# Two-layer transformer: a sequence's value sums are turned and divided in two steps instead of one

## What is computed

```python
# layer 0: 16 heads of 16, every head with its own keys and values
attn = jax.nn.softmax(jnp.einsum('gqd,gkd->gqk', q, k) * norm, axis=-1)
ctx = jnp.einsum('gqk,gkd->gqd', attn, v)
out = ctx @ Wproj.T + bproj
# layer 1: 16 heads, 4 groups of keys and values, causal
scores = jnp.where(causal[None, None, :, :], -jnp.inf, scores)
attn = jax.nn.softmax(scores, axis=-1)
out = jnp.einsum('bhqk,bhkd->bhqd', attn, v)
```

## Time and profile before

| | us |
|---|---|
| median of 3 runs | 715.38 |
| lowest and highest run | 715.2, 718.11 |
| the profiled execution (its span) | 734.3 |
| PE busy in it | 556.6 (76%) |
| DVE busy | 478.0 (65%) |
| ACT busy | 340.3 (46%) |
| POOL busy | 262.3 (36%) |

### The profile page before, as it was taken

One profiled execution on the slowest core, in us unless ns is written; L12 is line 12 of the kernel. 1 busy time (PEld: TensorE's weight loads), 2 busy tenths in 40 slices (PEclk: granted clock), 3 DMA queues, 4 the chain that ended last, 5 costly groups with the idle time before them and its releaser, 6 DMA issues.

```text
span 734.3 us, 14600 instructions
## 1 busy us (share of the span) xinstructions
PE 556.6 (76%) x4098; PEld 390.8 (53%) x4099; DVE 478.0 (65%) x1351; ACT 340.3 (46%) x870; POOL 262.3 (36%) x398
## 2 busy tenths in 40 slices
PE   4996669899796789788787877765589999899100
PEld 2653435565486555556565654543277777677100
DVE  4558548686158883757674852665757777677488
ACT  2541437577655546145653554530055555555100
POOL 1431001001411134245345243455436666566400
PEclk9997789999998899889989797866799999999655
DMA  7779967400000019693033051162434444444392
GB/s 222 197 245 243 215 135 211 141 2 4 1 1 1 1 55 246 162 241 139 3 112 137 16 203 53 37 244 88 130 96 138 143 145 143 136 140 134 130 409 84
DMA packets 50397, 95.19 MB, mean 130 GB/s; under 512 B 8676, under 2 KB 40620, under 8 KB 48556
## 3 DMA queue, kind: packets, MB, share of 16 engines
q1 hardware_dynamic: 41516, 71.14, 34.2%
q0 software_dynamic: 7680, 19.21, 7.1%
q10 hardware_dynamic: 1152, 4.19, 1.4%
HBM read 58.54 MB, written 35.59 MB: 128 GB/s over the span
## 4 chain that ended last, share of the span: by engine, by line
PE 47%; DVE 24%; DMA 7%; issue 7%; ACT 6%; another core or an unknown queue 4%; POOL 2%; SPq 1%; ACTq 0%; DVEq 0%; POOLq 0%
PE banks L1462 9%; PE banks L1252 5%; PE banks L1477 5%; DMA arena<-negT 4%; DVE arena L2029 4%; PE banks L1085 4%; PE banks L1208 4%; PE banks L1273 3%; DVE mx L1757 3%; DVE mx L1760 2%; PE banks L1449 2%; PE banks L1091 2%; PE banks L1153 2%; PE banks L1367 1%
## 5 line engine op out<-in xcount | busy, mean ns | idle before, releaser
L958 ACT ACTIVATE arena<-banks 128x512 f32<-128x512 f32 (+1 forms) x256 | 130.8, 547 | 118.7 <-PE banks L1252 75.7
L1252 PE MATMUL banks<-arena 98*128 98x256 bf16 (+1 forms) x512 | 93.5, 279 | 44.4 <-DMA arena<-negT 18.2
L1757 DVE TENSOR_REDUCE mx<-banks 128x4 f32<-128x1024 f32 x64 | 76.1, 1221 | 32.9 <-PE banks L1208 32.9
L1208 PE MATMUL banks<-arena 96*128 96x256 bf16 (+1 forms) x512 | 91.5, 285 | 6.0 <-DVE mx L1757 3.8
L814 POOL DMA_INDIRECT results_by_token<-attn_w,goes x80 | 80.2, 1002 | 35.2 <-issue 32.5
L1252 PEld LDWEIGHTS banks<-arena 98*128 98x128 bf16 x512 | 45.4, 105 | 80.5 <-DMA arena<-negT 19.7
L1462 PE MATMUL banks<-arena,attn_w 128*128 x320 | 84.1, 385 | 0.8 <-issue 0.5
L1760 DVE TENSOR_REDUCE mx<-banks 128x4 f32<-128x1024 f32 (+1 forms) x48 | 57.9, 1222 | 35.1 <-PE banks L1212 24.3
L776 POOL DMA_INDIRECT rows_by_expert<-arena,bpb x64 | 63.0, 984 | 27.5 <-issue 18.0
L1208 PEld LDWEIGHTS banks<-arena 96*128 96x128 bf16 x512 | 53.6, 107 | 25.2 <-issue 7.3
L1477 PE MATMUL banks<-arena,attn_w 128*128 x160 | 49.6, 392 | 11.4 <-issue 7.5
(11 more groups left out here) (231 smaller groups left out, 1110.0 us busy)
## 6 DMA issues: line engine op xcount, KB each, us to landing
arena<-parts_dram SPq DMA_DIRECT2D x72, 256.0 KB, 6.8
pvs<-rows_by_expert SPq DMA_DIRECT2D x80, 130.0 KB
parts_dram<-arena SPq DMA_DIRECT2D x24, 384.0 KB, 3.6
arena<-in SPq DMA_DIRECT2D x2, 2304.0 KB
rows_by_expert<-zero SPq DMA_DIRECT2D x1, 4160.0 KB, 22.8
arena<-results_by_token SPq DMA_DIRECT2D x8, 512.0 KB, 12.1
arena<-results_by_token ACTq DMA_DIRECT2D x8, 512.0 KB, 12.4
arena<-in SPq DMA_DIRECT2D x2, 1920.0 KB
```

The costliest lines, as they stand in the source:

```text
L958: act.activation(p_ring[n][:, i % P_RING, :], st_bank[RING_AT[n]["s", b, s] % 3][:, 0:P_WIDTH[n]], ACT.Exp, scale=HD ** -0.5).then_inc(exp ...
L1208: ins = pe.matmul(dst[:, a * nk:(a + 1) * nk], q_rows(n, slice(0, STACK), h0 + a, b, qt * P, P), k_rows(n, slice(0, STACK), h0 + a, b, 0, ...
L1252: ins = pe.matmul(dst[:, at:at + SEQ - q0], keys, q_rows(n, slice(0, ROWS), s, b, q0, SEQ - q0), start=True, stop=(n == 0 or b < POOL_MASKS))
L1757: ins = dve.tensor_reduce(out, src.rearrange("p (q h k) -> p q h k", q=QT, k=nk), AX.X, ALU.max)
```

## The change

`TURN` is now the pair of steps (5, 6). The first half of the sums is turned and divided at s = 5, in front of that step's unit of products on PE and of its reduction on DVE; the second half at s = 6, which has no unit, on PE behind the value sums of that step, on DVE as the first thing of it. `ring_uses` puts each half at its own step. What followed the second half on DVE in layer 1 still follows it. The last sequence of each layer is turned and divided at the end as before.

```diff
-TURN_MAX, COPY_MAX, TURN = 8, 9, 5
+TURN_MAX, COPY_MAX, TURN = 8, 9, (5, 6)
@@ ring_uses
             uses.append(("s", b, h))
-            if b and h == TURN:
-                uses += [("t", b - 1, q) for q in range(QT)]
+            if b and h in TURN:
+                uses.append(("t", b - 1, TURN.index(h)))
@@ PE
-            def turn_back(n, b):
+            def turn_back(n, b, qt):
                 pe.wait_ge(pvs_ready[n], (b + 1) * ROUNDS)
-                for qt in range(QT):
-                    wait_ring(n, ("t", b, qt))
-                    dst = st_bank[RING_AT[n]["t", b, qt] % 3]
+                wait_ring(n, ("t", b, qt))
+                dst = st_bank[RING_AT[n]["t", b, qt] % 3]
...
                             values(n, i // ROUND - 1)
+                        if b > 0 and s in TURN:
+                            turn_back(n, b - 1, TURN.index(s))
                         for at in pairs_at(n, i):
                             pair(n, *at)
-                        if b > 0 and s == TURN:
-                            turn_back(n, b - 1)
@@ DVE
-            def divide(n, b):
-                for qt in range(QT):
-                    dve.wait_ge(turned_back[n], b * QT + qt + 1)
+            def divide(n, b, qt):
+                dve.wait_ge(turned_back[n], b * QT + qt + 1)
...
-                if n == 1:
+                if n == 1 and qt == QT - 1:
                     dve.wait_ge(divided[1], (b + 1) * QT)
...
                     for s in range(HEADS):
+                        if b > 0 and s in TURN:
+                            divide(n, b - 1, TURN.index(s))
                         for at in pairs_at(n, b * HEADS + s):
                             pair(n, *at)
-                        if b > 0 and s == TURN:
-                            divide(n, b - 1)
```

More of the change, by code:

```diff
@@ L1281, in values @@
                 ins.then_inc(pv_ready[n], 1)
-            def turn_back(n, b):
+            def turn_back(n, b, qt):
                 pe.wait_ge(pvs_ready[n], (b + 1) * ROUNDS)
-                for qt in range(QT):
-                    wait_ring(n, ("t", b, qt))
-                    dst = st_bank[RING_AT[n]["t", b, qt] % 3]
-                    for grp in range(ROUNDS):
-                        ins = pe.transpose(dst[:, grp * P:(grp + 1) * P],
-                                           pvs[:, grp, qt * P:(qt + 1) * P], ident[:, :])
-                    ins.then_inc(turned_back[n], 1)
+                wait_ring(n, ("t", b, qt))
+                dst = st_bank[RING_AT[n]["t", b, qt] % 3]
+                for grp in range(ROUNDS):
+                    ins = pe.transpose(dst[:, grp * P:(grp + 1) * P],
+                                       pvs[:, grp, qt * P:(qt + 1) * P], ident[:, :])
+                ins.then_inc(turned_back[n], 1)
             def turn_rows(b):
@@ L1412, in attention @@
                 values(n, SEQS * ROUNDS - 1)
-                turn_back(n, SEQS - 1)
+                for qt in range(QT):
+                    turn_back(n, SEQS - 1, qt)
                 if n:
@@ L1842, in find_slots @@
                 dve.tensor_copy(slot[:, at, :], pk[1][:, at, :]).then_inc(slots_ready, 1)
-            def divide(n, b):
-                for qt in range(QT):
-                    dve.wait_ge(turned_back[n], b * QT + qt + 1)
-                    pv = st_bank[RING_AT[n]["t", b, qt] % 3].rearrange("p (h d) -> p h d", d=32)
-                    step(n, dve.reciprocal(rec[:, qt, :], pv[:, :, HD]))
-                    if n == 0:
-                        for e in range(2):
-                            heads = slice(e * SEQS, (e + 1) * SEQS)
-                            ins = dve.tensor_tensor(ctx0[:, :, qt, 2 * b + e, :],
-                                                    pv[:, heads, 0:HD],
-                                                    rec[:, qt, heads].unsqueeze(2).broadcast_to([P, SEQS, HD]),
-                                                    ALU.mult)
-                    else:
-                        ins = dve.tensor_tensor(att[:, qt, :].rearrange("p (h d) -> p h d", d=HD), pv[:, :, 0:HD],
-                                                rec[:, qt, :].unsqueeze(2).broadcast_to([P, HEADS, HD]), ALU.mult)
-                    ins.then_inc(divided[n], 1)
-                if n == 1:
+            def divide(n, b, qt):
+                dve.wait_ge(turned_back[n], b * QT + qt + 1)
+                pv = st_bank[RING_AT[n]["t", b, qt] % 3].rearrange("p (h d) -> p h d", d=32)
+                step(n, dve.reciprocal(rec[:, qt, :], pv[:, :, HD]))
+                if n == 0:
+                    for e in range(2):
+                        heads = slice(e * SEQS, (e + 1) * SEQS)
+                        ins = dve.tensor_tensor(ctx0[:, :, qt, 2 * b + e, :],
+                                                pv[:, heads, 0:HD],
+                                                rec[:, qt, heads].unsqueeze(2).broadcast_to([P, SEQS, HD]),
+                                                ALU.mult)
+                else:
+                    ins = dve.tensor_tensor(att[:, qt, :].rearrange("p (h d) -> p h d", d=HD), pv[:, :, 0:HD],
+                                            rec[:, qt, :].unsqueeze(2).broadcast_to([P, HEADS, HD]), ALU.mult)
+                ins.then_inc(divided[n], 1)
+                if n == 1 and qt == QT - 1:
                     dve.wait_ge(divided[1], (b + 1) * QT)
@@ L1898, in attention @@
                     add_soft(len(BATCHES) - 2)
-                divide(n, SEQS - 1)
+                for qt in range(QT):
+                    divide(n, SEQS - 1, qt)
                 if n:
```

## The result

| | before | changed |
|---|---|---|
| median of 20 runs each, alternating on one chip | 715.15 us (710.97 to 720.4) | 723.41 us (715.35 to 731.12) |
| profiled execution: span, granted clock | 716.4 us, 0.884 | 716.2 us, 0.886 |

The account below looks back on a forecast made before the run. PE (47% of the chain) and DVE (24%) taking turns in the attentions bound it; waits for divisions were 12.1 us. Terms -1.4 +1.3 -0.9 -0.3 +0.2 +1.3 = +0.2 on 715.38 gave 715.6 us, range 711.0 to 718.8.

Parts of the forecast that it names:

- Layer 0: Layer 0's attention: shorter PE stall, 0.22 us gained in each of four steady turns; -1.4 us kept for the layer.
- turns 1 and 3: Layer 0 turns whose copy of the sums is early enough not to be waited for: 0.3 us gained each.
- Layer 1, sequences 1 and 2: PE waits for the copy of the sums, delaying second reciprocal and statistics: +0.63 us each, +1.3 for both.
- Sequence 3: Layer 1: earlier first division brings scores 7 forward 1.6 us and closes DVE's 0.88 us hole: -0.9 us.
- Sequence 4: Layer 1: second division some 0.45 us earlier, beside a wait with no releaser: counted 0, -0.5 kept for the range.
- Sequences 5 and 6: Layer 1: 5 closes a 0.33 us DVE hole, -0.3; 6 has a late copy, +0.5, partly swallowed, counted +0.2.
- Sequence 7: Layer 1, no units left: second turning and reciprocal come later, behind value sums; PE waits for shared expert: +1.27 us.
- The second half is late everywhere: Rival: layer 1's statistics chain decides, each turn loses what turn 7 does; 724.3 us, or 720.4; chance 0.10.
- The first rival: PE's waits for the divisions come back, most of 12.1 us: 707.2 us, half of it 711.3; chance 0.12.
- The third: Rival: nothing changes hands; waits no instruction ends could move by 1 to 3 us: 713 to 718; 0.78 with forecast.

Follow-up runs that it names:

- e8: New order in layer 1 only, plus 8 unread score products at step 10 of layer 1's sequences 1 to 4; 743.81 us, 1.0008 to before.
- e9: Changed kernel (both layers) plus 8 unread score products at step 10 of layer 1's sequences 1 to 4; 742.23 us, 0.998 to before.
- e13: Changed kernel plus 8 unread score products at step 10 of layer 1's sequences 1 and 2 only; 724.68 us, 1.0127 to before.
- e14: Changed kernel plus 24 unread score products at step 10 of layer 1's sequence 3 only; 721.92 us, 1.0093 to before.
- e16: Changed kernel plus unread score products at step 10 of layer 1: 8 in sequences 1, 2 and 4, 24 in 3; 717.13 us, 1.0015 to before.
- before, again: The kernel before, unchanged, run once more for a second profile without the unexplained waits; 718.24 us, profiled span 716.4 us.
- e18: New order in layer 0 only, layer 1 as before, on a chip with unexplained waits; 743.26 us, 0.9996 to before.
- e7: New order in layer 0 and, in layer 1, only for the turn done during sequence 5; 740.82 us, 0.9967 to before.
- e15: The changed kernel unaltered, as control on the chip of the fourth batch; 725.62 us, 1.0034 to before.
- e1: New order in layer 0 only, layer 1 as before, in the first batch; 714.47 us, 0.9964 to before.
- e2: New order in layer 1 only, layer 0 as before; 724.83 us, 1.0074 to before.
- e3: The changed kernel unaltered, run again for a second profile in the first batch; 728.39 us, 1.0147 to before.
- e6: New order in layer 1 only for the second half (step 6), first half left behind step 5's unit; 744.52 us, 1.0027 to before.

## Why the prediction was wrong

**The step that failed** is that every hole of PE was priced at its own length. The sum has no term for the granted clock of the work behind a hole, and it puts sequence 4 at 0. The runs show that clock as most of the loss: 1.6 of the 2.3 us in a steady sequence (e8, e9, e13), 2.65 of the 3.7 us in sequence 4 (e14), and 8.5 of the 9.4 us between the medians when these holes are filled (e16).

**Layer 0: right.** -0.22 us a steady turn with a new wait of 0.39 for the copy; measured -0.27 with 0.37. The wait behind was put at 0.20, which with 0.39 does not add up to that gain; it is 0.10 (0.31 instead of 0.21 in front of L1240; in the last of these turns 0.53). The 0.3 us in each of turns 1 and 3 can't be seen: their distances vary by 1 us and more with either order. The layer-0-only kernels came out 3.1 and 0.8 us below before, around the 1.4 forecast; the second by itself is not clear of no change.

**Layer 1, sequences 1 and 2: mechanism right, one term missing.** I had the new wait at 0.78 (0.75), the second reciprocal 0.63 us later, and ACT and PE idle for it. From scores 10 of sequence 1 to the second reciprocal of sequence 2 it is 10.35 us in e16 and 9.80 in before, again: 0.55 later. With the holes filled the stretch is 0.73 us longer than before (15.70 against 14.97). But I wrote "ACT and PE idle there, so nothing hides it", and ended the sum there. The hole that grew from 1.03 to 1.62 us was followed by matmuls at 1.2 GHz, 1.6 us more. The sum used each row's duration as if the order did not touch it; the clock stood in it only as a property of the rows used.

**Sequence 3: wrong.** The gain of 0.9 us rested on DVE's hole of 0.88 us in front of the reduction at 374.66. In before, again, the same reduction has no idle time in front of it; in e18, with layer 1 as before, it has:

```profile
371.09 1.21 DVE L1760 TENSOR_REDUCE mx<-banks 128x8 f32<-128x1024 f32 x1
```
```profile
370.25 1.23 DVE L1767 TENSOR_REDUCE mx<-banks 128x8 f32<-128x1024 f32 x1 [0.87 <-PE banks L1217]
```

So the hole belongs to some executions of the old order (with the first half in its old place, 0.88 and 0.87 us in two of nine profiles, 0.30 in e7, none in six), and a term can't rest on one of them. Scores 7 did come earlier: PE's wait for the division is 1.70 us in e15 instead of 3.21, so 1.5 us shorter, where 1.6 was forecast. That PE then got idle time back as the 2.69 us in front of the ranks because DVE sets the time is argued, not tested. The stretch became 0.9 us longer instead. It holds the hole in front of scores 10 of sequence 2; with that hole filled (e8, e9, e13, e16) it is 22.2 to 22.3 us, against 22.91 in before, again, and 22.29 in e1, so a gain of the new order here is not shown either.

**Sequence 4: wrong by the largest amount.** I counted 0. It lost 3.7 us (16.81 to 20.54), 3.1 by the additions; the window of 9.72 against 7.01 us holds 2.7 of these. With the hole in front filled 1.1 us are left (17.89).

**Sequences 5 and 6: better than forecast.** -0.3 and +0.2 were counted. The stretches of 5 and 6 change by -1.8 and +0.6 (23.46 to 21.69, 16.75 to 17.39). PE's wait for the division in sequence 5 is 3.53 us in before, again, and 1.13 in e16; that this is what shortens the stretch was not tested by itself.

**Sequence 7: right.** +1.27 forecast; PE's wait for the shared expert grew from 2.64 to 3.80 us, +1.16. A part of that depends on the clock: where the stretch in front of it ran at 0.92 instead of 0.71, in e1, the old order already has 3.11, while the new one has 3.80 at either. e15, weight loads and DVE, then e1:

```profile
457.19 1.78 PEld L1366 LDWEIGHTS banks<-arena,attn_w 128*128 128x128 f32 x5 [3.80 <-DVE attn_w L1692]
...
451.04 0.26 DVE L1848 RECIPROCAL rec<-banks 128x16 f32<-128x16 f32 x1
...
453.03 0.26 DVE L1848 RECIPROCAL rec<-banks 128x16 f32<-128x16 f32 x1 [1.28 <-PE banks L1289]
```
```profile
450.76 2.89 PEld L1371 LDWEIGHTS banks<-arena,attn_w 128*128 128x128 f32 x8 [3.11 <-DVE attn_w L1699]
```

**The sum by measured terms** (e15 against before, again; spans 723.3 and 716.4): up to layer 1's first turning of maxima -2.6, of which the four steady turns of layer 0 are 1.1; the stretch of sequence 1 +1.5; the five stretches behind it +5.8; from there to the last turn +2.6, of which sequence 7's wait is 1.2; the rest -0.4. Together +6.9, beside 9.4 between the medians. The remainder, and the terms that I can't assign to an edit, lie in stretches that vary whatever the order. That of sequence 1 takes 15.0 to 18.6 us with layer 1 as before and 15.4 to 20.2 with the new order. The one from sequence 6's turning of the maxima to the additions of sequence 7 is 20.6 us at a clock of 0.92 or 23.65 at 0.71 with layer 1 as before, and 21.6 at 0.92 or 25.1 at 0.73 with the change. Of the profiles with the change, e2, e3, e13 and e15 had the long one, e14, e16 and the first one (the profiled execution of the result) the short one. One profile each does not settle how often the change brings the long one, and it stays open. The first one shows what this can hide: it has the same losses as e15 (sequence 2 17.24 us at 0.90, sequence 4 20.67 at 0.83), and its span is that of before, again, less 0.2 us because it is quicker behind them, 21.58 instead of 23.65 us to the additions of sequence 7 and 264.66 instead of 268.64 from there to the end.

**The rivals.** "The second half is late everywhere" gave 720.4 to 724.3 and had the right side at 0.10; its mechanism was not the cause: sequence 7 loses by the later half, and in sequence 2 the second half behind the value sums costs 0.2 us by itself (e6, 15.19). The first rival got nothing. The third took the waits of 12.64 us for a trait of the kernel; they belong to the first profile of before and to some chips. What the Trainium skill says of breaking up instructions (Perfetto Trace Analysis, "Optimizing Scalar/DVE Operations") is near to this change, which breaks up a group of them: the layer-0 turns got 0.27 us shorter and the stretch of sequence 5 1.8, but sequences 1 and 2 got longer where the earlier piece put a new wait of 0.75 us on PE.

## What to carry to other kernels

When an edit moves a wait on TensorE, do not stop at the wait's length: look at the granted clock of the stretch behind each hole that grows, and if it now reads 1.00, price the work that follows at the lower level as the upper bound. A wait that moves can cost more than it saves: here 3.21 us went, 2.69 came three steps later, and the sequence behind lost 3.7. Filling a hole with unread work tests this, but is no cure to count on: 24 products held the clock of sequence 4 twice, eight held it in e8 and not in e9. Take a second profile of the same kernel before resting a term on a single hole, above all when the profiled time is 19 us above the median.

## What the runs showed of the hardware

- A hole of PE longer by 0.59 us (1.62 instead of 1.03) was followed by a stretch with a granted clock of 0.78 instead of 1.00, and the same work took 7.70 instead of 6.15 us. At that place (scores 10 of sequence 1) every profile with a hole of 1.02 or 1.03 us shows a stretch of 14.95 to 15.19 us at 1.00, and those with 1.50 to 1.62 us 17.24 to 17.29 at 0.90, but for e14. The Trainium skill (TensorE: Matmul & The Clock Gate, "The HAM clock gate") says that the gate has two states and follows how busy PE has been, in a window whose phase is not tied to the kernel; e14's late fall and the clocks of the filled kernels agree with that, and no run here shows the window.
- Unread matmuls in such holes made a kernel quicker: 48 of them, and 8.5 us less in the median (725.62 to 717.13).
- The granted clock is not settled by one hole alone: in front of the ranks of sequence 3, holes of 1.21 us (e8) and 1.22 us (e9) were followed by a stretch of 20.42 us at 1.00 and one of 23.18 at 0.85.
- Three of the five chips of these batches made every kernel of this program some 27 us longer. 17 of 24.7 us between two profiles of the layer-0-only kernel had come by the additions of sequence 7 (447.36 and 464.18 us). Waits that end by nothing the profile shows stand there, up to 12.8 us on DVE; their cause was not tried. On the one of these chips where the changed kernel ran beside the kernel before, it cost 3.1 us instead of 9.4: sequence 4 is slow there without it, 21.2 to 22.8 us with the old order and 23.2 with the new.
